# Second attention of a vision tower: probabilities turned by transposing transfers, scores from two row tiles of TensorE, new queue orders

## What is computed

```python
qkv = x @ W_qkv                       # x: layer-normed h, (64, 197, 192); W_qkv: 192 x 2304
qkv = qkv.reshape(b, t, dh, 3, h)     # dh = 64, h = 12 heads
...
s = jnp.einsum('ghid,ghjd->ghij', q, k) * scale
a = jax.nn.softmax(s, axis=-1)
out = jnp.einsum('ghij,ghjd->ghid', a, v)
...
return out @ W_0                      # 768 x 192; added to h
```

## Time and profile before

| | |
|---|---|
| median of three runs | 2591.67 us |
| the profiled execution, its own time | 2584.25 us |
| its span, first to last instruction | 2582.4 us |
| PE, PEld busy | 95%, 80% |
| DVE, ACT, POOL busy | 82%, 81%, 42% |
| TensorE clock granted, mean | 0.992 of full speed |

### The profile page before, as it was taken

The page is one execution under the profiler, slowest core; times in us unless marked ns, Lnnn a source line. Parts: engine busy times, 40 slices in busy tenths (PEclk is TensorE's granted clock), DMA queues, the critical chain, the costliest instruction groups (busy, mean ns, idle before and its releaser), DMA issues. The chain is left out here.

```text
span 2582.4 us, 80520 instructions
## 1 busy us (share of the span) xinstructions
PE 2441.6 (95%) x26949; PEld 2055.8 (80%) x26949; DVE 2123.9 (82%) x5606; ACT 2082.3 (81%) x6129; POOL 1075.6 (42%) x1519
## 2 busy tenths in 40 slices
PE   5989999999998999999999999999999999998886
PEld 5778867888786888888888888888888888886554
DVE  5767668888876888888888888888888888887886
ACT  4777767777765888888888888888888888886997
POOL 5677733333331444444444444444444444442232
PEclk9999999999999999999999999999999999999999
DMA  5344401001002333333333333333333333330111
GB/s 177 112 112 118 115 20 29 4 5 41 14 5 59 85 72 70 83 72 70 83 72 70 83 72 70 83 72 70 83 72 70 83 72 70 83 72 16 49 49 56
DMA packets 185283, 175.16 MB, mean 68 GB/s; under 512 B 20423, under 2 KB 183857, under 8 KB 184945
## 3 DMA queue, kind: packets, MB, share of 16 engines
q1 hardware_dynamic: 185200, 174.14, 28.1%
HBM read 46.49 MB, written 9.68 MB: 22 GB/s over the span
## 5 line engine op out<-in xcount | busy, mean ns | idle before, releaser
L1499 POOL TENSOR_TENSOR b_pr<-b_pr,fc 128x394 f32<-128x394 f32 (+1 forms) x768 | 626.2, 840 | 962.0 <-DVE fc L1435 962.0
L1358 ACT ACTIVATE b_pr<-b_banks,fc 128x197 f32<-128x197 f32 (+1 forms) x1536 | 626.1, 422 | 35.2 <-DVE fc L1429 27.7
L1429 DVE TENSOR_REDUCE fc<-b_banks 128x2 f32<-128x394 f32 (+1 forms) x768 | 395.3, 556 | 63.7 <-PE b_banks L1280 60.0
L1264 PE MATMUL b_banks<-fp,wqkv 128*128 128x197 f16 x3840 | 383.2, 249 | 3.7 <-DVE b_qk L1419 2.4
L1290 PE MATMUL b_bank_t<-ident,b_pr 128*128 128x128 f32 (+3 forms) x3072 | 335.0, 250 | 17.2 <-DVE fp L1400 11.5
L1264 PEld LDWEIGHTS b_banks<-fp,wqkv 128*128 128x128 f16 x3840 | 314.6, 98 | 36.6 <-issue 18.9
L1280 PE MATMUL b_banks<-b_kst,b_qst 128*128 128x197 f16 (+1 forms) x3072 | 326.4, 248 | 2.1 <-ACT b_pr L1358 2.1
L1290 PEld LDWEIGHTS b_bank_t<-ident,b_pr 128*128 128x128 f32 (+3 forms) x3072 | 284.1, 141 | 50.7 <-issue 26.2
L1358 ACT ACTIVATION_READ_ACCUMULATOR b_pr<-b_banks,fc 128x1 f32 (+1 forms) x1536 | 311.6, 203 | 0.0
L1280 PEld LDWEIGHTS b_banks<-b_kst,b_qst 128*128 128x128 f16 (+1 forms) x3072 | 264.9, 105 | 21.6 <-issue 11.7
L1419 DVE SCALAR_TENSOR_TENSOR b_qk<-b_banks,b_qk 128x394 f16<-128x394 f32 x384 | 215.7, 562 | 48.0 <-ACT b_qk L1343 48.0
(11 more groups left out here) (254 smaller groups left out, 4741.7 us busy)
## 6 DMA issues: line engine op xcount, KB each, us to landing
b_qst<-b_qk SPq DMA_DIRECT2D x512, 147.8 KB, 2.6
b_kst<-b_qk SPq DMA_DIRECT2D x512, 73.9 KB, 2.3
patches<-in_x SPq DMA_DIRECT2D x64, 588.0 KB, 4.3
out<-z_res SPq DMA_DIRECT2D x64, 96.0 KB
m_raw_weights<-in_wqkv SPq DMA_DIRECT2D x2, 1152.0 KB, 6.7
out<-z_res SPq DMA_DIRECT2D x32, 51.8 KB
h<-h SPq DMA_DIRECT2D x32, 44.2 KB
out<-z_res SPq DMA_DIRECT2D x32, 44.2 KB
```

What stands on the lines that cost most here:

```text
L1264: last = t.matmul(out[:, g * SEQ:(g + 1) * SEQ], w[:, (2 * n + g) * P:(2 * n + g + 1) * P], x, start=(j == 0), stop=(j == 4))
L1358: last = nc.scalar.activation(pr[n % 3][0:ROWS[c], c, e, :], banks[0:ROWS[c], c, e * SEQ:(e + 1) * SEQ], ACT.Exp, bias=nmx[n % 2][0:ROWS[c ...
L1429: v.reduce_max(nmx[n % 2][0:ROWS[c], c, :], banks[0:ROWS[c], c, 0:2 * SEQ].rearrange("p (e t) -> p e t", e=2), AX.X, negate=True).then_inc ...
L1499: last = nc.gpsimd.tensor_tensor(p, p, inv, ALU.mult)
```

## The change

All in `attention_1` (a helper gets its engine as an argument, with no effect):

- Scores no longer need stacked operands: the two heads of a pair lie in partitions 0 to 63 and 64 to 127 of `b_qk`, and are multiplied there by weights of 64 rows x 128 columns, in two row tiles, three products each. `b_qst`, `b_kst` and their 16 transfers are gone. A pair takes 12 matmuls, the two heads taking turns, each head in a PSUM bank of its own, and there are two sets of banks for scores. The four banks that this takes come from the f32 transposes and the old scores.
- The t steps are gone. ACT's new step **h** makes the high half of the probabilities from SBUF to SBUF (two ACTIVATE), a new step **l** the low half (two tensor_tensor): on DVE for pairs 0, 1, 3 and 4, on POOL for 2 and 5. Then SP issues two `dma_start_transpose` for a pair: 128 rows, and 80 rows, of 1024 f16 each (2 halves, 2 heads, 256 keys, of which 197 are real), which write `b_pt` with keys in the partitions.
- `b_halves` is a ring of three pairs: h of pair n waits until the transfers of pair n-3 have landed. e of pair n waits for the low half of n-3.
- All four orders are new; mixing (m on PE) and projection (w) stand up to a round later than before.

```diff
+    FLIP_ROWS = (P, TAIL + 11)
+    QUERIES = sum(FLIP_ROWS)
+    PE_ORDER = ("m5^^ v2 s5^ q5 w^^ s0 x' v3 m0^ s1 m1^ m2^ q0' s2 q1' q2' m3^ s3 "
+                "v0' q3' m4^ s4 q4' v1'").split()
+    ACT_ORDER = ("e2 v0' q3' o1^ e3 q4' h1 v1' o2^ h2 v2' e4 q5' e5 h3 h4 v3' x'' "
+                 "e0' o0 h5 q0'' e1' q1'' q2'' h0'").split()
+    DVE_ORDER = ("v1 o2^^ v2 m5^ r4^ n' q5 w^^ r5^ l3^ m0 v3 x' l4^ r0 m1 q0' o0^ m2 "
+                 "r1 q1' q2' l0 m3 v0' r2 q3' m4 o1^ r3 q4' l1").split()
+    POOL_ORDER = ("p1 p2 l2 p3 k^ p4 p5 p0' l5").split()
...
-        kst = sb("b_kst", [P, 2, PAIRS, SEQ], F16)
-        qst = sb("b_qst", [P, 2, 2, PAIRS, SEQ], F16)
+        halves = [sb(f"b_halves{r}", [P, 2, 2, 2, 2 * P], F16) for r in range(3)]
+        pt = [sb(f"b_pt{r}", [P, 2, 2, 2, QUERIES], F16) for r in range(2)]
...
-        banks = ps("b_banks", [P, 4, 512])
-        bank_t = ps("b_bank_t", [P, 2, 512])
+        banks = ps("b_banks", [P, 2, 512])
+        scores = [ps(f"b_scores{r}", [P, 2, 512]) for r in range(2)]
...
                     elif kind == "s":
-                        pe.wait_ge(stacked[n // 3], STACK * (img + 1))
+                        pe.wait_ge(qk_split, PAIRS * img + n + 1)
+                        for e in range(2):
+                            if later(PAIRS * img + n - 1):
+                                pe.wait_ge(freed[e], PAIRS * img + n - 1)
                         for c in range(2):
-                            if later(PAIRS * img + n):
-                                pe.wait_ge(freed[c], PAIRS * img + n)
-                            for e in range(2):
-                                for part in range(2):
-                                    last = t.matmul(banks[0:ROWS[c], c, e * SEQ:(e + 1) * SEQ], qst[:, part, e, n, COLS[c]],
-                                                    kst[:, e, n, :], start=(part == 0), stop=(part == 1))
-                            last.then_inc(ready[c], 1)
-                    elif kind == "t":
...
+                            for j, (pa, pb) in enumerate(PARTS):
+                                for e in range(2):
+                                    rows = slice(e * DH, (e + 1) * DH)
+                                    last = t.matmul(scores[n % 2][0:ROWS[c], e, c * SEQ:(c + 1) * SEQ], qk[rows, n, pa, 0, COLS[c]],
+                                                    qk[rows, n, pb, 1, :], start=(j == 0), stop=(j == 2))
+                        last.then_inc(ready, 1)
                     elif kind == "m":
-                        pe.wait_ge(pt_split, PAIRS * img + n + 1)
+                        pe.wait_ge(*turned(img, n))
...
+                    elif kind == "h":
+                        act.wait_ge(prob_made, PAIRS * img + n + 1)
+                        if later(PAIRS * img + n - 2):
+                            act.wait_ge(*turned(img, n - 3))
+                        for c in range(2):
+                            copy(halves[n % 3][0:ROWS[c], c, 0, :, 0:SEQ], pr[n % 3][0:ROWS[c], c]).then_inc(high_made, 1)
...
+                    elif kind == "l":
+                        for c in range(2):
+                            dve.wait_ge(high_made, 2 * (PAIRS * img + n) + c + 1)
+                            low(halves[n % 3][0:ROWS[c], c, 1, :, 0:SEQ], pr[n % 3][0:ROWS[c], c],
+                                halves[n % 3][0:ROWS[c], c, 0, :, 0:SEQ]).then_inc(low_by_v, 1)
...
+                def step(n, img, odd):
+                    for c in range(2):
+                        sp.wait_ge(*low_made(img, n, c))
+                        if later(PAIRS * img + n - 3):
+                            sp.wait_ge(mixed, PAIRS * img + n - 3)
+                        at, rows = c * P, FLIP_ROWS[c]
+                        sp.dma_start_transpose(pt[(2 * odd + n) % 4][:, :, :, :, at:at + rows].rearrange("p a e k t -> p (a e k) t"),
+                                               halves[n % 3][0:rows, c].rearrange("p a e k -> p (a e k)")).then_inc(flipped[n % 3], 16)
...
+                for r in range(3):
+                    last = nc.gpsimd.memset(halves[r][:], 0.0)
...
+                    if kind == "l":
+                        for c in range(2):
+                            pool.wait_ge(high_made, 2 * (PAIRS * img + n) + c + 1)
+                            nc.gpsimd.tensor_tensor(halves[n % 3][0:ROWS[c], c, 1, :, 0:SEQ], pr[n % 3][0:ROWS[c], c],
+                                                    halves[n % 3][0:ROWS[c], c, 0, :, 0:SEQ], ALU.subtract).then_inc(low_by_p, 1)
+                        return
```

More of the change, by code:

```diff
@@ L1115, in job_bank @@
     def job_bank(kind, n):
-        return 2 + [(s[0], number(s)) for s in JOBS].index((kind, n)) % 2
+        return [(s[0], number(s)) for s in JOBS].index((kind, n)) % 2
     def job_before(s, i):
@@ L1178, in at, with low_made, turned @@
             return (0, P)[c] if not odd else (TAIL, 0)[c]
-        gathered = qk[:].rearrange("p a g n t -> p (a g n t)")[:, 0:2 * PAIRS * sum(rows_left)].rearrange("p (k t) -> p k t", k=2 * PAIRS)
-        def left_columns(m):
-            return slice(sum(rows_left[0:m]), sum(rows_left[0:m + 1]))
+        slots = [qk[:, 2 * m:2 * m + 2].rearrange("p n a g t -> p (n a g t)") for m in range(3)]
+        gathered = [slots[m][:, 0:2 * PAIRS * rows].rearrange("p (k t) -> p k t", t=rows) for m, rows in enumerate(rows_left)]
+        def low_made(img, n, c):
+            before, n = divmod(n, PAIRS)
+            signal, by = (low_by_p, LOW_ON_POOL) if n in LOW_ON_POOL else (low_by_v, LOW_ON_VECTOR)
+            return signal, 2 * len(by) * (img + before) + 2 * by.index(n) + c + 1
+        def turned(img, n):
+            return flipped[n % 3], 32 * (2 * img + n // 3 + 1)
         def made(s, img):
@@ L1203, in round_of @@
                         step(s, s[0], number(s), i + ahead(s), like, (like + ahead(s)) % 2)
-            first, end = 1 - min(shifts), n_img - max(shifts)
+            first, end = max(2, 1 - min(shifts)), n_img - max(shifts)
             turns = max(0, (end - first) // 2)
@@ L1229, in mix_left @@
                         for j, (pa, pb) in enumerate(PARTS):
-                            last = t.matmul(out, gathered[:, pa * PAIRS + f, left_columns(m)], S["wo"][:, pb, f, :], start=(f == 0 and j == 0), stop=(f == PAIRS - 1 and j == 2))
+                            last = t.matmul(out, gathered[m][:, pa * PAIRS + f, :], S["wo"][:, pb, f, :], start=(f == 0 and j == 0), stop=(f == PAIRS - 1 and j == 2))
                     last.then_inc(left_ready, 1)
@@ L1241, in step @@
                     if isinstance(img, int) and img == 0 and (kind, n) in first_steps:
-                        work(first_steps[kind, n], out if s in JOBS else banks[:, 0])
+                        work(first_steps[kind, n], out if s in JOBS else scores[1][:, 0])
                     if isinstance(img, int) and img == n_img - 1 and (kind, n) in last_steps:
-                        if kind == "t":
+                        if kind == "m":
                             pe.wait_ge(h_updated, img)
@@ L1316, in step @@
                         last.then_inc(job_made, 1)
+                for r in range(2):
+                    for e in range(2):
+                        work(1, scores[r][:, e])
                 run(pe, PE_ORDER, step)
[L1319 removed]
+                for c in range(2):
+                    pe.wait_ge(freed[c], PAIRS * n_img)
                 pe.wait_ge(left_gathered, 3)
[L1321 to L1322 removed]
+                mix_left(2, scores[0][0:rows_left[2], 0, 0:D])
+                work(3, scores[1][:, 1])
             @block.scalar
@@ L1340, in step @@
                     elif kind == "q":
-                        if n % 3 == 0 and later(img):
-                            act.wait_ge(stacked[n // 3], STACK * img)
-                        nc.scalar.activation(qk[:, 0, :, n], banks[:, k, 0:2 * SEQ].rearrange("p (g t) -> p g t", g=2), ACT.Copy,
+                        if later(img):
+                            act.wait_ge(ready, PAIRS * (img - 1) + n + 1)
+                        nc.scalar.activation(qk[:, n, 0], banks[:, k, 0:2 * SEQ].rearrange("p (g t) -> p g t", g=2), ACT.Copy,
                                              scale=QK_SCALE).then_inc(qk_hi, 1)
@@ L1467, in _ @@
                 run(dve, DVE_ORDER, step)
-                add_left(2, bank_t[:, 0, 0:D])
+                add_left(2, scores[0][:, 0, 0:D])
             @block.sync
             def _(sp):
-                def step(s, kind, a, img, like, odd):
-                    sp.wait_ge(qk_split, PAIRS * img + 3 * a + 3)
-                    pairs = slice(3 * a, 3 * a + 3)
-                    for e in range(2):
-                        head = slice(e * DH, (e + 1) * DH)
-                        for half in range(2):
-                            rows = slice(half * DH, (half + 1) * DH)
-                            sp.dma_start(qst[rows, :, e, pairs, :], qk[head, :, 0, pairs, :]).then_inc(stacked[a], 16)
```

(6 more changed lines are left out.)

126 lines of the change are left out of this document (49 added, 77 removed).

## The result

The changed kernel takes 2527.7 us (2524.18 to 2529.86), the kernel before 2592.0; ratio 0.975, interval 0.973 to 0.977. 64 us were gained where 133 were forecast. The direction and the wide range held; the likeliest case's own range (2408 to 2517) did not.

A forecast was written before the change was run, and what follows sets the result against it. PE bound the kernel at 24.19 us a round; with ACT and DVE then level, 22.0 us gains 140 us, less 8 at the ends: 2452 profiled, 2459 us as median; likeliest 2408 to 2517, wide 2380 to 2840.

The forecast's parts named there:

- the wide range: Whole kernel: 2380 to 2840 us, leaving out a little over half of the case of transposing transfers as bound.
- the likeliest case's own range: Second attention: ACT and DVE bind at 21.2 to 22.9 us a round, 2408 to 2517 us; chance 0.50.
- PE: Second attention: t steps gone, scores in row tiles; busy time falls from 24.0 to 20.2 us a round.
- rival (c): Score matmuls: the row tiles take turns and PE stays the bound, 23.0 us a round, 2524 us; chance 0.08.
- ACT: Second attention: twelve copies now SBUF to SBUF, 0.04 us dearer each; busy 20.8 to 21.3 us a round.
- POOL: Second attention: multiplications plus four low halves, 13.7 us a round, under 18 with blocking; not a bound.
- Transfers: Twelve transposes a round: below 20 us, between 11.7 by bytes and 46 by pieces; a pair's landing in 4.6 us.
- DVE: Second attention: low halves from SBUF, with 1.6 us of exclusion by POOL; busy 21.2 us a round.
- The sum: ACT 21.3 and DVE 21.2 us level, plus 0.6 for the wait for l5: round 22.0, gain 140, less 8.
- rival (b): Second attention: nearly no waits, little exclusion; ACT alone at 20.8 us a round or less, 2383 us and below; chance 0.10.
- the wait for l5: POOL's low half of pair 5 ends about 0.6 us after ACT wants the exp that needs it; one visible wait.
- Ends: First and last image of the stage, with mixing placed a round later: some 8 us more in all.

The follow-up runs named there:

- the last order: Changed kernel with normalisation moved behind v0, where POOL idles, v3 before x, l3 before r5 and l0 before r1: 2390.6 us, ratio 0.924 to the kernel before.

## Why the prediction was right or wrong

**PE: right, the last digit by luck.** 20.2 us busy forecast, 20.2 measured; s at 0.62 us where 0.63 was taken. That leaves rival (c) out, although its time, 2524, is nearest to the measured one: PE is not the bound, and its tiles don't take 1.0 us. In the last order, at a clock of 1.00, the same steps are busy 19.6 us. The lower clock was priced at nothing and came to 0.14 us a round.

**ACT: 0.7 high.** 21.3 forecast, 20.6 measured, so it was not level with DVE; busy 89% where over 93% was named as a sign of being right.

**POOL: right.** 13.7 and blocking forecast, 14.3 measured.

**Transfers: right where it mattered.** Under 20 us a round, landing about 4.6, was the value; the 16 engines are busy 0.589 x 23.08 = 13.6 us a round with them, the queue takes 15.6, and they land in 3.2. The reason given, that a small piece costs less than a packet of 1 KB, held (21 against 74 ns), but what would bind is the issue on SP's queue, 1.3 us each, which I had not priced at all. Of the two figures of the Trainium skill weighed there, 261 GB/s ("DMA: Bandwidth & Descriptors", Latency and other measured facts) made 9.8 us where the trace has 13.6. The other, 1309 ns for one 128x128 block ("VectorE: DVE Perf Modes", The three transpose paths), is no rate: here eight blocks are issued every 1.3 us.

**DVE: the step that failed.** The low halves were priced well, 553 + 200 ns against 738 measured. But the same exclusion was not carried to the other instructions of DVE that work from SBUF. The normalisation takes 2 x (949 + 607) - 4 x 335 = 1.8 us a round more, and it stood in no term of my sum. I had read POOL's even 837 to 845 ns in the attention as a sign that only DVE's subtractions contend; in truth the normalisation stood in the old order where POOL idled, and the new order puts it behind r4, into POOL's run p3, p4. The orders were in the change; what I had not done is lay the two new queues beside each other. The Trainium skill names tensor_scalar, in its 2-port modes, among the instructions that contend with GpSimd, and says that a tensor_tensor with two SBUF inputs contends with GpSimd's reads and not with an instruction that only writes ("SBUF — State Buffer", Who interferes with whom). The run in which POOL mostly writes agrees on both: 620 and 431 ns for the one, 560 for the other.

**The sum.** With 1.8 more, DVE would be 23.0 and the round 23.8; measured are 22.3 busy and 23.1. The 0.7 between are, start to start in the two traces: low halves of q and v 0.3 shorter in the fuller queue (which I had given to rival (b)), the twelve low halves that went 5.8 us and not 5.6, the eight that came 5.3 and not 5.4, and a slip of 0.1 (21.3 - 5.6 + 3.8 is 19.5, not 19.6). The allowance between busy time and round, 0.8, came out, but by luck: 0.6 of it was the wait for l5, which does not exist. Ends 13 us for 8. (The upper end of the wide range is 2843 by its own sum, not 2840, which decides nothing.)

**What the sum could not have shown.** That 1.8 us a round are not 115 us. Taken away alone they brought 10. The runs show a loop: two thirds of any small addition to DVE or ACT reach the end, and a removed hold-up lets DVE come to the next one earlier. With all three meetings gone (normalisation, l3, l0), and v3 moved, 137 us come back, and the round is 20.96, near ACT's busy time, close to my rival (b). That is 2.1 us a round, of 3.2 that DVE loses at the meetings (1.8 at the normalisation, 8 x 0.178 = 1.4 at the subtractions). Why the meetings cover for each other is argued from two profiles (l3 rose to 2.55 us when the normalisation was gone); it was not isolated further. Which wait closes the loop in the changed kernel stays open. One candidate stands in its list of waits: ACT waits 1.7 us a round for v3, which stands on PE behind x, which waits for q5's low half behind the normalisation.

**Counting the 0.6 us of l5** as a visible wait was wrong: ACT waits for no low half in the changed kernel (0.8 of the 30.1 us idle in front of exp is for anything but the maxima, of 1000).

## What to carry to other kernels

Before summing what an engine has to do, lay the queues of VectorE and GpSimd beside each other: each instruction of one that reads SBUF twice, or is a tensor_scalar from SBUF, against what the other is doing, or released to do, at that moment. Try the semaphore that starts GpSimd behind, not in front of, the VectorE instruction that would exclude it, and VectorE's other such instructions where GpSimd idles; with the small changes of place beside them these moves brought 137 us here, the whole change 64. And when several hold-ups lie in one loop, taking one away proves little: try them together before dropping the theory.

## What the hardware showed that was not expected

- A transposing transfer of up to 128 x 1024 f16, SBUF to SBUF, takes 1.25 us of its queue (1.3 from issue to issue), no less with 48 rows than with 128, and lands 3.2 us after issue; a packet of it costs 21 ns on an engine (0.589 x 16 x 1000 us / 448196).
- An f32 tensor_scalar of 128 x 128, 335 ns alone, reached 1739 ns beside GpSimd's multiplications of 840 ns, since it waited until two of them had ended, and is held up by memsets as well (620 and 431 ns in the mean); a tensor_tensor with two SBUF inputs is not held up by memsets (560 ns).
- Matmuls of 64 rows in two row tiles keep their pace without alternating between the tiles: 12 of 197 columns in 0.62 us either way, where 8 of 128 rows took 0.68.
- TensorE's clock did not fall behind an idle time of 0.95 us in any of 22 rounds; behind 2.5 us it fell in 13 of 21, and not in the other 8.
